# The scan stores its results in token order, and the outputs stage works on token tiles with block matmuls

## What is computed

```
def step(state, inp):
    q_t, k_t, v_t, a_t, b_t = inp
    state = a_t[..., None, None] * state
    stored = jnp.einsum('bhij,bhj->bhi', state, k_t)
    delta = b_t[..., None] * (v_t - stored)
    state = state + jnp.einsum('bhi,bhj->bhij', delta, k_t)
    o_t = jnp.einsum('bhij,bhj->bhi', state, q_t)
    return (state, o_t)
...
var = jnp.mean(out * out, axis=-1, keepdims=True)
out = out * jax.lax.rsqrt(var + 1e-06) * rms_w
gate = jax.nn.silu(x @ Wgate)
return out * gate @ Wout
...
x = x + ga * _L0_attn_ref(h, ...)
```

## Time and profile before

| | |
|---|---|
| median of 3 runs | 4078.28 us |
| lowest, highest | 4064.94, 4079.76 us |
| the profiled execution: its span | 4095.8 us |
| scan, first to last decay | 931.1 to 1427.4 us |
| outputs stage, first DMA issue to that of the next stage | 1433.87 to 1916.49 us |
| share of the span that each engine is busy | PE 65%, DVE 56%, ACT 30%, POOL 13% |

### The profile page before, as it was taken

One profiled execution on the slowest core, in us unless ns is written; L12 is line 12 of the kernel. 1 busy time (PEld: TensorE's weight loads), 2 busy tenths in 40 slices (PEclk: granted clock), 3 DMA queues, 4 the chain that ended last, 5 costly groups with the idle time before them and its releaser, 6 DMA issues. The chain is left out here.

```text
span 4095.8 us, 91128 instructions
## 1 busy us (share of the span) xinstructions
PE 2662.8 (65%) x34356; PEld 1876.5 (46%) x34356; DVE 2279.2 (56%) x5483; ACT 1247.2 (30%) x3021; POOL 537.4 (13%) x613
## 2 busy tenths in 40 slices
PE   5986775238888846554666468877783009999900
PEld 2554544235555523333333345555552009999800
DVE  3385565725666568886711447666777014444457
ACT  3664453225666501110400024333441002222200
POOL 1221111000000001110000001100110660000076
PEclk8997776555555578777777588888895559999955
DMA  3536465653333284402097542112110532222265
GB/s 111 184 139 239 173 243 179 235 204 98 104 101 102 89 211 124 124 21 77 28 382 321 223 165 69 54 54 67 54 61 23 182 98 66 70 70 71 65 183 175
DMA packets 411029, 536.53 MB, mean 131 GB/s; under 512 B 178740, under 2 KB 339728, under 8 KB 401424
## 3 DMA queue, kind: packets, MB, share of 16 engines
q1 hardware_dynamic: 350832, 369.32, 28.1%
q0 software_dynamic: 39616, 127.22, 8.6%
q10 hardware_dynamic: 20320, 36.44, 2.4%
HBM read 327.84 MB, written 216.15 MB: 133 GB/s over the span
## 5 line engine op out<-in xcount | busy, mean ns | idle before, releaser
L1031 ACT ACTIVATE ss_write_ps<-ss_state,ss_gammas 128x64 f32<-128x64 f32 x1024 | 263.3, 303 | 195.7 <-DVE ss_state L1079 195.7
L453 PE MATMUL dc_rows_ps<-dc_weights,dc_hT 128*128 128x512 f32 x512 | 290.9, 697 | 7.9 <-issue 5.0
L1203 PE MATMUL do_late_ps<-do_scratch,do_ident 128*128 128x512 f32 (+1 forms) x416 | 197.1, 631 | 109.8 <-DVE do_scratch L1238 109.8
L2556 PE MATMUL se_up_ps<-se_xT,se_w 128*128 128x128 f32 x2176 | 267.3, 276 | 0.1
L510 PE MATMUL dc_solve_ps<-dc_sides,dc_blocks 32*32 32x32 f32 x8192 | 124.3, 226 | 217.6 <-ACT dc_blocks L604 100.5
L2564 PE MATMUL se_y_ps<-se_w,se_aT 128*128 128x256 f32 x1088 | 257.2, 379 | 0.0
L2556 PEld LDWEIGHTS se_up_ps<-se_xT,se_w 128*128 128x128 f32 x2176 | 255.8, 193 | 0.5 <-DVE se_w L2621 0.4
L2621 DVE COPY se_w<-mx_weights 128x2048 f32 x136 | 166.7, 1227 | 100.5 <-issue 100.5
L510 PEld LDWEIGHTS dc_solve_ps<-dc_sides,dc_blocks 32*32 32x32 f32 x8192 | 111.3, 139 | 231.5 <-issue 118.3
L2694 POOL DMA_INDIRECT cb_y<-scratch_ys,cb_to x128 | 135.3, 1057 | 573.9 <-DVE cb_to L2708 531.0
L2564 PEld LDWEIGHTS se_y_ps<-se_w,se_aT 128*128 128x128 f32 x1088 | 196.4, 190 | 21.1
(11 more groups left out here) (346 smaller groups left out, 5655.5 us busy)
## 6 DMA issues: line engine op xcount, KB each, us to landing
ex_w<-in_w_all SPq DMA_DIRECT2D x64, 1024.0 KB
scratch_rows<-dc_rows POOLq DMA_DIRECT2D x64, 512.0 KB, 4.1
scratch_vw<-dc_out POOLq DMA_DIRECT2D x64, 512.0 KB, 4.5
dc_c_rows<-scratch_rows SPq DMA_DIRECT2D x64, 384.0 KB, 4.5
scratch_xs<-wa_zeros ACTq DMA_DIRECT2D x34, 512.0 KB, 12.6
se_xs<-scratch_xs SPq DMA_DIRECT2D x136, 128.0 KB, 2.1
scratch_ys<-se_y SPq DMA_DIRECT2D x136, 128.0 KB
ss_wq_rows<-scratch_vw SPq DMA_DIRECT2D x128, 128.0 KB, 2.2
```

The lines of the kernel that those rows point to most:

```text
L453: mm = pe.matmul(to, hT[n % 2][:, k, :], weights[:, k, columns], start=(k == 0), stop=(k == HALVES - 1), skip_group_check=True)
L1031: ins = act.activation(write_ps[b][:, k, 0:WIDTH], state[b][:, k, :], ACT.Copy, scale=gammas[i][:, b, k, c:c + 1])
L1203: mm = pe.matmul(late_ps[:, to:to + (2 - skip) * DIM], ident[:, :], scratch[lag % 2][:, (t + skip - lag) * DIM:(t + 2 - lag) * DIM], start ...
L2556: mm = pe.matmul(up_ps[i % 2][:, c * P:(c + 1) * P], w[i % (2 * AHEAD)][:, k * DFF + c * P:k * DFF + (c + 1) * P], xT[i % 2][:, k, :], sta ...
```

## The change

**Scan.** `uqs` is replaced by two DRAM tensors in token order, `solved_u` and `solved_q`, each 8192 x 256. A batch element's part of a tile is now stored by eight DMAs (four units, u and read), each from 16 partitions with 8 pieces of 64 floats. They are issued by POOL after DVE's last subtraction of the tile (`u_ready`), 16 to a tile, and SP issues no store any more. `out_done` counts from zero and DVE's first pair of tiles is written out ahead of its loop.

**Outputs stage.** 16 quads (`Q` = 4 tiles of 128 tokens, a token to a partition), in halves `m` of two tiles. ACT spreads the weights `qkd` of two tiles into blocks of 32x32 (L1249), two chunks to a block with the other chunk's part set to zero by `parity`. The sum within a chunk is one matmul for each head and each 32 tokens (L1203). DVE adds what the query read, ACT squares, DVE sums, normalizes and multiplies by the gate. `rms_w`, `w_out` and `ga` are multiplied once into `w_gated`, so POOL's multiplication and DVE's by `ga` are gone. SP issues the loads, POOL the stores of x1. The loops over quads are written out.

```diff
 build_state_scan
-        STORES = BATCH * 16
-        uqs_v = d["uqs"].rearrange("u a t c f -> (u a t) c f")
+        STORES = 2 * UNITS * BATCH * 16
+        solved_v = [d[name].rearrange("(b i c t) f -> b i t c f", b=BATCH, c=N, t=CHUNK) for name in ("solved_u", "solved_q")]
-                def store(tile, i):
-                    for b in range(BATCH):
-                        sync.dma_start(uqs_v[:, bass.ds(tile * N + b * (CHUNKS // BATCH), N), :], solved[i][:, b, :, :]).then_inc(out_done[i], 16)
+            @block.gpsimd
+            def _(pool):
+                def store(tile, i):
+                    for b in range(BATCH):
+                        pool.wait_ge(u_ready[b], at((tile + 1) * N))
+                        for u in range(UNITS):
+                            for a in range(2):
+                                lines = slice(u * QUAD + a * CHUNK, u * QUAD + (a + 1) * CHUNK)
+                                to = solved_v[a][b, bass.ds(tile, 1), :, :, unit_column(u):unit_column(u) + WIDTH].rearrange("a t c f -> (a t) c f")
+                                pool.dma_start(to, solved[i][lines, b, :, :]).then_inc(out_done[i], 16)
+                with pool.Fori(0, PAIR) as ii:
+                    for i in both:
+                        store(ii * 2 + i, i)
 build_delta_outputs
+                def load(q):
+                    i = q % 2
+                    if q >= 2:
+                        sync.wait_ge(mixed, at((q - 1) * 2))
+                        sync.wait_ge(summed, at((q - 1) * 2))
+                    sync.dma_start(qkd[i][:, :, :], quad_rows(d["qkd"], q)).then_inc(first_in[i], 16)
+                    sync.dma_start(u[i][:, :, :], quad_rows(d["solved_u"], q)).then_inc(first_in[i], 16)
+                    sync.dma_start(read[i][:, :, :], quad_rows(d["solved_q"], q)).then_inc(first_in[i], 16)
+                    if q >= 2:
+                        sync.wait_ge(o_ready, at(q - 1))
+                    sync.dma_start(gate[i][:, :, :], quad_rows(d["rows"], q)[:, :, 3 * DIM:4 * DIM]).then_inc(gate_in[i], 16)
+                    if q >= 2:
+                        sync.wait_ge(x_out[i], q // 2 * 16)
+                    sync.dma_start(x[i][:, :, :], quad_rows(d["x"], q)).then_inc(x_in[i], 16)
...
+                for q in range(QUADS):
+                    pool.wait_ge(x_ready, at((q + 1) * 2))
+                    pool.dma_start(quad_rows(d["x1"], q), x[q % 2][:, :, :]).then_inc(x_out[q % 2], 16)
...
+                def mix(m):
+                    q, half = divmod(m, 2)
+                    if half == 0:
+                        pe.wait_ge(first_in[q % 2], at((q // 2 + 1) * 48))
+                    for n in range(2):
+                        for h in range(HEADS):
+                            for j in range(4):
+                                tokens = slice(32 * j, 32 * j + 32)
+                                mm = pe.matmul(mix_ps[m % 2][tokens, n, h * HEAD:(h + 1) * HEAD], blocks[m % 2][tokens, n, h, :, :].rearrange("p c t -> p (c t)"),
+                                               u[q % 2][tokens, half * 2 + n, h * HEAD:(h + 1) * HEAD], start=True, stop=True, skip_group_check=True)
+                    mm.then_inc(mixed, 1)
...
+                def project(m):
+                    pe.wait_ge(weights_ready, at(1))
+                    pe.wait_ge(oT_ready, at(m + 1))
+                    if m >= 2:
+                        pe.wait_ge(x_ready, at(m - 1))
+                    b = m * BATCH // PAIRS_OF_TILES
+                    for n in range(2):
+                        for k in range(HALVES):
+                            mm = pe.matmul(y_ps[m % 2][:, n, :], oT[m % 2][:, n, k, :], w_gated[:, b, k, :], start=(k == 0), stop=(k == HALVES - 1))
...
+                for q in range(QUADS + 1):
+                    if q < QUADS:
+                        mix(2 * q)
+                        mix(2 * q + 1)
+                    if q > 0:
+                        turn(2 * q - 2)
+                        turn(2 * q - 1)
+                        project(2 * q - 2)
+                        project(2 * q - 1)
...
+                def make_blocks(m):
+                    q, half = divmod(m, 2)
+                    if half == 0:
+                        act.wait_ge(first_in[q % 2], at((q // 2 + 1) * 48))
+                    if m >= 2:
+                        act.wait_ge(mixed, at(m - 1))
+                    for par in range(2):
+                        ins = act.activation(blocks[m % 2][:, :, :, par, :].rearrange("p n h t -> p (n h) t"),
+                                             pair_of(qkd[q % 2], half).rearrange("p (a t) -> p a t", t=T), ACT.Copy, scale=parity[:, par:par + 1])
+                    ins.then_inc(blocks_ready, 1)
...
+                for q in range(QUADS + 1):
+                    if q > 0:
+                        square(q - 1)
+                        root(q - 1)
+                    if q < QUADS:
+                        silu(q)
+                    if q + 1 < QUADS:
+                        make_blocks(2 * q + 2)
+                        make_blocks(2 * q + 3)
+                    if q > 0:
+                        copy_turned(2 * q - 2)
+                        copy_turned(2 * q - 1)
...
+                for b in range(BATCH):
+                    for k in range(HALVES):
+                        seq.done(vec.scalar_tensor_tensor(w_gated[:, b, k, :], w_out[:, k, :], rms_w[:, 0:1], ga[:, b, :], ALU.mult, ALU.mult))
...
+                def normalize(q):
+                    heads = o[q % 2][:, :, :].rearrange("p n (h e) -> p (n h) e", e=HEAD)
+                    vec.wait_ge(squared, at(q + 1))
+                    seq.wait()
+                    seq.done(vec.tensor_reduce(rms[:, 0, :], squares[:, :, :].rearrange("p n (h e) -> p (n h) e", e=HEAD), AX.X, ALU.add))
+                    seq.wait()
+                    seq.tell(vec.tensor_scalar(rms[:, 0, :], rms[:, 0, :], 1.0 / HEAD, 1e-6, ALU.mult, ALU.add), var_ready, q + 1)
+                    vec.wait_ge(rooted, at(q + 1))
+                    seq.done(vec.reciprocal(rms[:, 1, :], rms[:, 1, :]))
+                    seq.wait()
+                    vec.wait_ge(summed, at((q + 1) * 2))
+                    seq.done(vec.tensor_tensor(heads, heads, spread(rms[:, 1, :], HEAD), ALU.mult))
+                    seq.wait()
+                    vec.wait_ge(silued, at(q + 1))
+                    seq.tell(vec.tensor_tensor(o[q % 2][:, :, :], o[q % 2][:, :, :], gate[q % 2][:, :, :], ALU.mult), o_ready, q + 1)
...
+                for q in range(1, QUADS + 1):
+                    normalize(q - 1)
+                    if q < QUADS:
+                        add(2 * q)
+                        add(2 * q + 1)
+                    add_x(2 * q - 2)
+                    add_x(2 * q - 1)
```

More of the change, by code:

```diff
@@ L946, in tile_pair @@
                             load(tile + 2, i)
-                        store(tile, i)
                 for i in both:
@@ L1108, in build_delta_outputs @@
         sem = Semaphores(nc, ctx, "do_")
+        both = range(2)
         ident = sb("ident", [P, P])
+        parity = sb("parity", [P, 2])
         w_out = sb("w_out", [P, HALVES, DIM])
[L1111 to L1117 removed]
@@ new lines, in build_delta_outputs @@
+        qkd = [sb(f"qkd{i}", [P, Q, DIM]) for i in both]
+        gate = [sb(f"gate{i}", [P, Q, DIM]) for i in both]
+        x = [sb(f"x{i}", [P, Q, DIM]) for i in both]
+        o = [sb(f"o{i}", [P, Q, DIM]) for i in both]
+        squares = sb("squares", [P, Q, DIM])
+        rms = sb("rms", [P, 2, Q * HEADS])
+        blocks = [sb(f"blocks{i}", [P, 2, HEADS, 2, T]) for i in both]
+        oT = [sb(f"oT{i}", [P, 2, HALVES, P]) for i in both]
+        mix_ps = [ps(f"mix_ps{i}", [P, 2, DIM]) for i in both]
@@ L1133, in build_delta_outputs, with quad_rows, pair_of @@
+        x_out = [sem.from_zero(f"x_out{i}") for i in both]
+        CONSTS = 16 * (4 + BATCH)
+        def quad_rows(dram, q):
+            return dram.rearrange("(q n p) f -> q p n f", n=Q, p=P)[q]
+        def pair_of(tile, half):
+            return tile[:, half * 2:half * 2 + 2, :].rearrange("p n f -> p (n f)")
         sem.start()
@@ new lines, in _ @@
+                for b in range(BATCH):
+                    sync.dma_start(ga[:, b, :], mod_row(d, 0, b * GROUPS_PER_BATCH, MOD_GA)).then_inc(consts, 16)
+                for q in range(1, QUADS):
+                    load(q)
+            @block.gpsimd
+            def _(pool):
+                for q in range(QUADS):
+                    pool.wait_ge(x_ready, at((q + 1) * 2))
+                    pool.dma_start(quad_rows(d["x1"], q), x[q % 2][:, :, :]).then_inc(x_out[q % 2], 16)
+                for i in both:
+                    pool.wait_ge(x_out[i], QUADS // 2 * 16)
@@ L1179, in _ @@
-            @block.gpsimd
-            def _(pool):
-                pool.wait_ge(consts, at(48))
-                with pool.Fori(0, GROUPS // 2) as r:
-                    for parity in both:
-                        g = r * 2 + parity
```

(16 more changed lines are left out.)

202 lines of the change are left out of this document (69 added, 133 removed).

## The result

The changed kernel takes **4016.8 us** (median of 4, 4014.57 to 4019.74) against 4079.02 of before on the same chip: ratio 0.9853, 95% interval 0.9833 to 0.9873, or 62 us less. The forecast was 4018. The profiled execution has a span of 4018.1.

The account below looks back on a forecast made before the run. The prediction took a ring through the loads, 24.9 us a quad, to bound the new outputs stage: 414 us against 482.6, −69. With +9 at the scan's end the sum is −60, forecast 4018 us, range 3945 to 4090.

Parts of the forecast that it names:

- the start: Outputs stage up to its first landed store: first loads and constants 11.3, blocks, two mixes 13.2 and more, 49 us.
- the end of the scan: Last tile's 16 POOL stores lie exposed after the scan's last step, landing 11.5 us after it: +9 us.
- the thirteen turns: Outputs stage after its first landed store: 13 turns of 24.9 us, 324 us.
- loads: In each turn, x, qkd, u and read, 2 MB at 348 GB/s plus latency: 8.5 us, bounds 7.9 and 10.
- projection: PE's two projection halves for a quad's four tiles, priced a little under the 1.2 GHz cost of 8.2: 7.0 us.
- the ring: Outputs stage: loads, block writes, copy, projection, residual and store wait on each other across SP and ACT, 24.9 us a quad.
- last two turns: End of the outputs stage, with no load to wait for: 23 and 16 us.
- Rival 2: Outputs stage: PE gets the fast clock (projection 3.8) or loads overlap better, 21.7 us a quad, 3966 us; chance 0.25.
- PE's path: PE alone per quad: rest of projection 7.6, mix 13.2, transposes 2.2, copy 0.6: 23.6 us, 1.3 inside the ring.
- DVE, POOL, scan: DVE 114 us for the outputs stage; POOL's 0.57 us issues hidden in the scan, whose step stays 1.95 us.
- Rival 3: Outputs stage: PE's instruction supply is the bound, 4.3 us a burst, PE path 27.6: 4064 or 4078 us; chance 0.12.
- Rival 4: POOL's queue paces the scan at 16c + 2.4 a tile, c one issue's price: 4108 to 4256 us; chance 0.13.

Follow-up runs that it names:

- e1: Changed kernel with ACT copying the transposed tiles of the previous quad before writing the next quad's blocks: 3977.8 us, ratio 0.9759 to the kernel before.
- e2: Changed kernel with SP issuing the load of x after the first loads of the next quad: 3986.0 us, ratio 0.9771 to the kernel before.
- e3: Changed kernel with half the block matmuls, one for two heads (sums of odd heads wrong): 3987.5 us, ratio 0.9776 to the kernel before.
- e5: Changed kernel with both the edits of e1 and e2: 3985.9 us, ratio 0.9769 to the kernel before.
- e10: e5 with every block matmul issued twice, 512 a quad: 4213.8 us, ratio 1.0332 to the kernel before.
- e6: Changed kernel with the scan's last stores on three queues and fewer waits for constants at the outputs stage's start: 4005.0 us, ratio 0.9822.
- e4: Changed kernel with each scan store issued twice on POOL, 32 a tile: 4139.1 us, ratio 1.0150 to the kernel before.
- e8: Changed kernel with the edits of e6 and e7 together: 3899.3 us, ratio 0.9566 to the kernel before.
- e12: e8 measured once more: 3903.8 us, ratio 0.9562 to the kernel before.
- e9: e5 with loads of qkd, u and read cut to one of four tiles from quad 2 on (output differs): 3965.4 us, ratio 0.9723.
- e7: e5 with blocks of 64x64 in place of 32x32, 128 block matmuls a quad: 3917.5 us, ratio 0.9588 to the kernel before.

## Why the prediction was right

It was right in mechanism and in sum (-60 forecast, -62 measured). That the sum came within 2 us is in part luck: the start was 12 too low and the end of the scan 4, and the thirteen turns were 11 too high and the last two 8.

| term, us | predicted | measured |
|---|---|---|
| loads, from the landed store to ACT | 8.5 | 10.3 |
| four block writes, copy | 3.3 | 3.1 |
| projection | 7.0 | 5.3 |
| last residual, store landed, hops | 6.1 | 5.4 |
| one turn of the ring | 24.9 | 24.1 |
| first store landed | 49 | 60.8 |
| thirteen turns | 324 | 313 |
| last two turns | 39 | 31.4 |
| last store landed, to the next stage | 2 | 3.2 |
| stage | 414 | 408.4 |
| end of the scan | +9 | +13.1 |

- **The ring** was read from the order of ACT and SP alone. ACT's 139.3 us behind `do_read` are its mark, and e1, e2, e3 and e5 show it: either cut frees the same quad, and half of PE's mixing changes it by 0.4.
- **Loads** were too cheap: 10.3 in the turn of the table, 9.5 to 10.8 and 10.1 in the mean over thirteen, at the upper bound of 10. What the sum left out is the load of the gate, which moves in the same stretch (2.63 MB in place of 2.1); at the 348 GB/s of the earlier trace rows it is worth 1.5 us, and 8.5 + 1.5 is 10.0. That is an estimate; no run left the gate out.
- **Projection** was priced at nearly the 1.2 GHz level, and a granted clock near 0.5 was one of the signs. It did not come: the stage had 0.63 in the mean, at times 0.50 (1602.5 to 1604.5 us) and at times 1.00 (1594 to 1598), and four tiles took 5.3 (4.4 to 6.6). Rival 2 needed 3.8.
- **PE's path.** The earlier trace rows was read rightly: 3.3 for 64 block matmuls, where the gap goes with their number (3.47 in e10); loads stretched it to about 3.6 (from the end of one projection to the next transposes 9.8 to 15.9 us in the changed kernel, mean of eleven 14.6). The path was said to lie 1.3 inside the ring; e1 makes it 2.6. Its 7.6 for the rest of a projection priced at 7.0 seems to count the copy twice; without that it is 23.0, 1.9 inside. The row that the prediction names for two tiles projected in 1.89 stands in the trace before (at 1904.89 us) but not in the earlier trace rows, which has one tile in 1.03. The sum used neither, rival 2 the 1.89.
- **Start** was too low by 12. The blocks came 15.25 us in, behind `do_ga`, the last constant (11.3 assumed); e6 recovers 7.5 of it on ACT and 5.0 at the first store. And the sum has the mixes of one quad, 13.2, where PE's queue has those of quad 1 as well ahead of the first transposes (e3: 13.9 less at the first store with half of them).
- **Last two turns**: 23 and 16 were assumed, 18.7 and 12.7 measured. These are quads without the ring and its loads, the last also without mixes.
- **DVE, POOL, scan** came as said: DVE was busy for 113.9 us (114 forecast), POOL took 0.528 to issue plus up to 0.1 between two (0.57), and the step was 1.953.
- **End of the scan**: the issues were priced rightly (e6 takes ten away and gains 6.0). The 4 us too few lie between the last issue and the next stage.
- **Rival 3** came in small: it is the bound once the ring is cut (e1, e10).
- **Rival 4** did not come, and its price was wrong: e4 rules out 16c + 2.4, and by its second reading c = 1.0 would give (15.6 + 2.4 + 16) / 2 = 17.0 us a tile, not 18.4, an estimate that no run tested at this c. The Trainium skill (SBUF — State Buffer, A bandwidth-pool intuition that's wrong (but worth ruling out)) has 3.1 us for a DMA of this queue beside a DVE copy; here no issue of 512 took over 0.572, with DVE busy 298 of 498 us, 63 of them with copies.

## What to carry to other kernels

Follow in-order queues for a ring before adding up engines: here no engine was busy for more than 54% of the stage, and one exchange of two calls on ACT was worth 39 us. Small matmuls that PE runs in a long straight line are paid by the instruction more than by their size: half as many with blocks of 64x64 took 23% off a quad that PE held. Stores moved to a queue that nobody waits for are free in the loop as long as their issues fit into a tile (16 did, the 32 of e4 did not), and cost their whole length after the last step. All edits together (e8, e12) give 0.956 of the kernel before.

## What the hardware showed that was not expected

- 64 block matmuls of 32x32 take 3.3 to 3.6 us at best from the start of one burst to that of the next, however fast the burst runs, and up to 7.0 while loads move. In the rows of e10 and e9 a burst works 1.90 us and the gap is 1.57 to 2.32; a faster burst of the changed kernel, 1.34 for 127 records, comes with a longer gap, and the next one starts 3.57 later:

```profile
1598.98 1.34 PE L1203 MATMUL do_mix_ps<-do_u,do_blocks 32*32 32x16 f32 x127 [2.46 <-issue]
...
1602.55 1.91 PE L1203 MATMUL do_mix_ps<-do_u,do_blocks 32*32 32x16 f32 x128 [2.23 <-issue]
```

  So a faster clock need not have helped the mixes. That the gap is the arrival of the next instructions is inferred, from e10 (it goes with their number, with one packet of instructions to a burst and no other traffic), e9 (loads stretch it) and e7 (none with half the number). A burst whose instructions had already arrived was not tried.
- With PE busy 199.97 of 200 us (e7) the granted clock was 0.70. The Trainium skill (TensorE: Matmul & The Clock Gate, Part 1) has sustained activity release the slow clock; this stretch bears it out in part only.
- The end of the scan, from its last issue to the next stage, grew from 4.7 to 9.7 us, and stayed at 8.4 when POOL issued none of the last stores. What it is stays open: a stage in which POOL issues no store at all was not tried.
- The row of L1241 in the kernel before, which the prediction calls inflated (2.4 us in the mean), is inflated by four single instructions. Here is one addition without POOL's work beside it, then POOL's multiplication and an addition of the same size beside it:

```profile
1468.73 2.29 DVE L1241 TENSOR_TENSOR do_o<-do_o,do_scratch 128x2048 f32<-128x2048 f32 x1
...
1578.14 10.64 POOL L1187 TENSOR_TENSOR do_gate<-do_gate,do_rms_w 128x4096 f32<-128x4096 f32 x1 [88.27 <-ACT do_gate L1171]
...
1580.14 10.79 DVE L1241 TENSOR_TENSOR do_o<-do_o,do_scratch 128x2048 f32<-128x2048 f32 x1
```

  Once in each of the four groups a DVE addition that starts beside POOL's multiplication ends only 1.6 to 2.2 us after it, about its own length, and takes 8.5 us more than otherwise, 34 us in all. So one of the two engines can hold up the other, although POOL's DMA issues in the scan show nothing of it. The change removes POOL's multiplication and with it these waits. By an estimate from them, folding `rms_w` into `w_out` alone would have taken up to 34 us off the old stage; no run changed it alone.
